# A fused token, recurrence and expert kernel on Trainium2: outputs of two expert pairs added on VectorE before the transpose, and the gate in one pass

## What is computed

```python
h = _L0_tok_ref(x, ...)                       # 1024 queries of 64 channels per batch
h = jnp.concatenate([h, txt], axis=1)         # 1152 tokens per batch
h = h + _L0_attn_ref(_layernorm(h), ...)      # recurrence over the 16 batches
h = h + _L0_ffn_ref(_layernorm(h), ...)

def _L0_ffn_ref(x, gate_w, gate_b, w1, w2, w3):
    logits = jnp.einsum('bsd,de->bse', x, gate_w) + gate_b
    top_probs, top_idx = jax.lax.top_k(jax.nn.softmax(logits, axis=-1), 2)
    top_probs = top_probs / jnp.sum(top_probs, axis=-1, keepdims=True)
    dispatch = jnp.sum(jax.nn.one_hot(top_idx, 16) * top_probs[..., None], axis=-2)
    hidden = jax.nn.silu(jnp.einsum('bsd,edh->bseh', x, w1)) * jnp.einsum('bsd,edh->bseh', x, w2)
    expert_out = jnp.einsum('bseh,eho->bseo', hidden, w3)
    return jnp.einsum('bseo,bse->bso', expert_out, dispatch)
```

## Time and profile before

| | us |
|---|---|
| median of 3 runs | 2227.41 (2227.31 to 2228.99) |
| the profiled execution's own time | 2234.98 |
| its span, first to last instruction | 2233.2 |
| PE busy | 2042.9 |
| DVE busy | 1842.9 |
| POOL busy | 1453.0 |
| ACT busy | 1121.3 |
| mean granted clock of TensorE | 0.972 |

### The profile page before, as it was taken

One profiled execution on the slowest core, in us unless ns is written; L12 is line 12 of the kernel. 1 busy time (PEld: TensorE's weight loads), 2 busy tenths in 40 slices (PEclk: granted clock), 3 DMA queues, 4 the chain that ended last, 5 costly groups with the idle time before them and its releaser, 6 DMA issues.

```text
span 2233.2 us, 42161 instructions
## 1 busy us (share of the span) xinstructions
PE 2042.9 (91%) x13857; PEld 1544.3 (69%) x13857; DVE 1842.9 (83%) x4580; ACT 1121.3 (50%) x2472; POOL 1453.0 (65%) x1657
## 2 busy tenths in 40 slices
PE   2468899999999999999999999999999999999989
PEld 1356677767677777767677776767777676777655
DVE  1336898989889898989989898998988899898886
ACT  1225455555555555555555555555545555544443
POOL 0378888577675758767575776857576785758600
PEclk9768999999999999999999999999999999999999
DMA  8787656366663647666464666646466665522200
GB/s 194 212 237 190 188 143 198 96 188 190 168 175 115 193 122 202 179 174 192 119 186 110 196 176 174 197 132 177 112 187 171 181 195 145 165 81 79 59 3 6
DMA packets 363271, 346.58 MB, mean 155 GB/s; under 512 B 49456, under 2 KB 313776, under 8 KB 362928
## 3 DMA queue, kind: packets, MB, share of 16 engines
q1 hardware_dynamic: 313904, 209.60, 34.8%
q0 software_dynamic: 49152, 134.28, 20.3%
HBM read 205.90 MB, written 137.89 MB: 154 GB/s over the span
## 4 chain that ended last, share of the span: by engine, by line
PE 78%; DVE 12%; issue 7%; ACT 2%; DMA 1%; POOL 1%; DVEq 0%; POOLq 0%; SPq 0%; ACTq 0%
PE bank_h L650 12%; PE bank_o L659 12%; PE bank_h L651 10%; PE bank_d L750 10%; PE bank_d L740 10%; PE bank_z L669 5%; PE bank_p L686 4%; PE bank_a L762 4%; DVE hid L1025 2%; PE bank_p L705 2%; DVE v_sb L1160 2%; DVE v_sb L1153 2%; PE bank_a L775 2%; PE bank_p L704 1%; PE bank_p L710 1%
## 5 line engine op out<-in xcount | busy, mean ns | idle before, releaser
L596 POOL DMA_INDIRECT gath<-table,idx x1024 | 1122.1, 1096 | 278.3 <-issue 238.6
L650 PE MATMUL bank_h<-xsplit,w 128*128 128x384 f32 x1536 | 589.6, 384 | 13.4 <-DVE hid L1025 12.4
L651 PE MATMUL bank_h<-xsplit,w 128*128 128x384 f32 x1536 | 521.0, 339 | 0.0
L834 ACT ACTIVATE silu<-bank_h 128x384 f32<-128x384 f32 x768 | 382.3, 498 | 262.1 <-PE bank_h L651 250.4
L1025 DVE TENSOR_TENSOR hid<-silu,bank_h 128x384 f32<-128x384 f32 x768 | 415.9, 549 | 58.1 <-ACT silu L834 51.7
L650 PEld LDWEIGHTS bank_h<-xsplit,w 128*128 128x128 f32 x1536 | 293.0, 191 | 113.0 <-issue 66.5
L1125 DVE TENSOR_TENSOR wsam<-gath,cw 128x1024 f32<-128x1024 f32 x256 | 312.9, 1222 | 43.9 <-PE bank_d L740 23.5
L659 PE MATMUL bank_o<-hid,w_sb 128*64 128x384 f32 x1536 | 335.2, 515 | 14.5 <-DVE scaled L1032 13.2
L616 POOL TENSOR_TENSOR lns<-lns,neghalf 128x3 f32<-128x3 f32 x96 | 88.7, 924 | 336.9 <-DVE lns L1004 335.5
L651 PEld LDWEIGHTS bank_h<-xsplit,w 128*128 128x128 f32 x1536 | 293.9, 191 | 3.2
L740 PE MATMUL bank_d<-eye,wsam 128*128 128x128 f32 x2048 | 278.1, 280 | 15.3 <-DVE wsam L1125 13.6
(11 more groups left out here) (157 smaller groups left out, 2559.8 us busy)
## 6 DMA issues: line engine op xcount, KB each, us to landing
table<-pixmaj SPq DMA_DIRECT2D x80, 1024.0 KB, 10.3
xin<-x_dram SPq DMA_DIRECT2D x256, 256.0 KB
table<-pixmaj SPq DMA_DIRECT2D x32, 960.0 KB
table<-pixmaj SPq DMA_DIRECT2D x16, 1088.0 KB
gath<-table,idx POOLq DMA_INDIRECT x1024
out_dram<-ob SPq DMA_DIRECT2D x48, 96.0 KB, 6.7
gath<-w_dram SPq DMA_DIRECT2D x4, 512.0 KB, 9.0
interp_sb<-interp_dram SPq DMA_DIRECT2D x1, 1024.0 KB, 5.0
```

The lines of the kernel that those rows point to most:

```text
L596: pool.indirect_dma_start(out=gath[buf][:, p, :, :].rearrange("p a c -> p (a c)"), out_offset=None, in_=table[par], in_offset=bass.Indirec ...
L650: mm(bank[:, 0:GC], w12[:, e, which, 0, :], xsplit[gp][:], start=True, stop=False)
L651: mm(bank[:, 0:GC], w12[:, e, which, 1, :], xsplit[gp][:], start=False, stop=True).then_inc(ready, 1)
L834: nc.scalar.activation(silu[e % 2][:], bank_h[r][:, 0:GC], ACT.Silu).then_inc(silu_done, 1)
```

## The change

Three things are changed. DVE adds the second of two neighbouring `scaled` tiles into the first after every second W (a new add of 128 x 384 whose both inputs are in SBUF, with a wait on DVE's own `eo_scaled` ahead of it), so that Z transposes two tiles in place of four. The gate weights' two parts are laid side by side, so that P7 is 3 matmuls of 32 columns in place of 6 of 16; their sum is now made by a second small add on DVE. And the strings of all engines in `ORDER` are new.

```diff
@@ Z on PE @@
-                        pe.wait_ge(eo_scaled, n + HALF)
+                        pe.wait_ge(eo_paired, (n + HALF) // 2)
                         wait(pe, mix_v, 4 * (NGRP * b + g) + 2 * half)
                         for k in range(GT):
-                            for q in range(HALF):
+                            for q in range(0, HALF, 2):
                                 last = mm(bank_z[:, 128 * k:128 * (k + 1)], scaled[(n + q) % SB][:, 128 * k:128 * (k + 1)],
-                                          eye[:], start=q == 0, stop=q == HALF - 1, is_transpose=True)
+                                          eye[:], start=q == 0, stop=q == HALF - 2, is_transpose=True)
@@ P7 on PE @@
-                            for part in range(2):
-                                last = mm(bank_p[:, NE * k:NE * (k + 1)], xsplit[gp][:, 128 * k:128 * (k + 1)],
-                                          gate_r[:, part, :], start=part == 0, stop=part == 1)
+                            last = mm(bank_p[:, 2 * NE * k:2 * NE * (k + 1)], xsplit[gp][:, 128 * k:128 * (k + 1)],
+                                      gate_r[:].rearrange("p a e -> p (a e)"), start=True, stop=True)
@@ W on DVE @@
                         tt(scaled[n % SB][:], bank_o[:, 0:GC], wide[:, q, :], ALU.mult).then_inc(eo_scaled, 1)
+                        if q % 2:
+                            dve.wait_ge(eo_scaled, n + 1)
+                            even = scaled[(n - 1) % SB]
+                            tt(even[:], even[:], scaled[n % SB][:], ALU.add).then_inc(eo_paired, 1)
@@ P7 on DVE @@
-                        link(top, tt(logit[:], bank_p[:, 0:GT * NE].rearrange("p (k e) -> p k e", k=GT),
-                                     spread(gateb[:], 1, GT), ALU.add))
+                        parts = bank_p[:, 0:2 * GT * NE].rearrange("p (k a e) -> p k a e", k=GT, a=2)
+                        link(top, tt(logit[:], parts[:, :, 0, :], spread(gateb[:], 1, GT), ALU.add))
+                        link(top, tt(logit[:], parts[:, :, 1, :], logit[:], ALU.add))
@@ ORDER, DVE's string, its first line @@
-        "efhjkkmkmnkmmknkmkmnkemkmfnhEjkFGmmknsktumkvmwnkyxzmkmAnJJJIkJJJmIkmJnIEJIFkGksmmJntJuJkJqIvewmkymJn",
+        "efhjkkmkmnkmkmnkmkmnkmkmenEfkFhGmmknsjktukmvmwnkyxzmkmAnJJJIkJJJmIkmJnIEJFkGksmmJntJuIkJJvqwIJkymJIm",
```

More of the change, by code:

```diff
@@ L192 @@
[L192 to L195, removed]
+        "aaaaaaaaaaaaaaaabbbbbbbbcdehiaaaaaaalalmmlaaalammllmmaalaabbbbbbbblcmdmellmhmilaltmumvalaalxmazJmaJl",
@@ new lines @@
+        "aBaJDIDJaDJlDJmDImDJIlDJDaJIJaalmmlJtJuKvlIJmJImxJlJzIaalaBmDJmDJIlDJaDJKDIDJbDJlDImtJmulvJIbbbbbbbJ",
+        "lJImJcmdxeJIKlJzJlIJmJImBJDlDJDIDlDJmDJDIDKmtJluJIJvlJIhmiJmJIaaJxaJIKaJzIJaaJaJaIBJDJDDIDlDJIDJKDlD",
+        "JmtJIumJvlJIJlaJImJxmJKIlJzIlJamJIJBmDaJDlJDIDalDJaDmJDKIDmtJauJlIaJlvIJamJbmbJIbbJbbbxbJcIKlJzIJlJd",
+        "mJImBJeDlDJDIDlDJmDJDIDKmtJluJIJvlJIhmiJmJIaaaJxaJIKJzaIJaaJaJIBJDJDDIDlDJKDJIDlDJmtJIumJvlJIJlaJImJ",
+        "xmJKIlJzIlJamJIJBmDaJDlDJIDalDJaDmJDKIDmtJauJlIaJlvIJamJbmbJIbbJbbbbxJcIKdlJzIJlJemJIBmDJlDJDIDlDJmD",
@@ new lines @@
+        "JDIDKmtJluJIJvlJIhmiJmJIaaJxaJIKaJzIJaaJaJaIBJDJDIDlDJIDJKDlDJmDJItmuJlvJIJlaJImJxmJKIlJzIlJamJIJBmD",
+        "aJDlJDIDalDJaDmJDKIDmtJauJlIaJlvIJamJbmbJIbbJbbbxbJcIKlJzdlJIJmJImBJeDlDJDIDlDJmDJDIDKmtJluJIJvlJIhm",
+        "iJmJIaaJxaJIKaJzIJaaJaJaIBJDJDIDlDJIDJKDlDJmDJItmuJlvJIJlaJImJxmJKIlJzIlJamJIJBmDaJDlJDIDalDJaDmJDKI",
+        "DmtJauJlIaJlvIJamJbmbJIbbJbbbxbJcIKlJzdlJIJmJImBJeDlDJDIDlDJmDJDIDKmtJluJIJvlJIhmiJmJIaaJxaJIKaJzIJa",
+        "aJaJaIBJDJDDIDlDJKDJIDlDJmtJIumJvlJIJlaJImJxmJKIlJzIlJamJIJBmDaJDlJDIDalDJaDmJDKIDmtJauJlIaJlvIJamJb",
@@ new lines @@
+        "mbJIbbJbbbbxJcIKdlJzIJlJemJIBmDJlDJDIDlDJmDJDIDKmtJluJIJvlJIhmiJmJIaaJxaJIKaJzIJaaJaJaIBJDJDIDlDJIDJ",
+        "KDlDJmDJItmuJvlJIJalJImJxmJKIlJzIlJamJIJBmDaJDlJDIDalDJaDmJDKIDmtJauJlIaJlvIJamJbmbJIbbJbbbxbJcIKlJz",
+        "dlJIJmJImBJeDlDJDIDlDJmDJDIDKmtJluJIJvlJIhmiJmJIaaJxaJIKaJzIJaaJaJaIBJDJDDIDlDJDKJDIDltJmuJImJvlJIJl",
+        "aJImJxmJKIlJzIlJamJIJBmDaJDlJDIDalDJaDmJDKIDmtJauJlIaJlvIJamJbmbJIbbJbbbbxJcIKdlJzIJlJemJIBmDJlDJDID",
+        "lDJmDJDIDKmtJluJIJvlJIhmiJmJIaaJxaJIKaJzIJaaJaJaIBJDJDDIDlDJKDJIDlDJmtJIumJvlJIJlaJImJxmJKIlJzIlJamJ",
@@ new lines @@
+        "IJBmDaJDlJDIDalDJaDmJDKIDmtJauJlIaJlvIJamJbmbJIbbJbbbxbJcIKlJzIJlJdmJImBJeDlDJDIDlDJmDJDIDKmtJluJIJv",
+        "lJIhmiJmJIaaJxaJIKaJzIJaaJaJaIBJDJDDIDlDJIDJKDlDJmtJIumJvlJIJlaJImJxmJKIlJzIlJamJIJBmDaJDlJDIDalDJaD",
+        "mJDKIDmtJauJlIavlJIJamJbmbJIbbJbbbbxJcIKdlJzIJlJemJIBmDJlDJDIDlDJmDJDIDKmtJluJIJvlJIhmiJmJIaaJxaJIKa",
+        "JzIJaaJaJaIBJDJDDIDlDJIDJKDlDJmtJIumJvlJIJlaJImJxmJKIlJzIlJamJIJBmDaJDlJDIDalDJaDmJDKIDmtJauJlIaJlvI",
+        "JamJbmbJIbbJbbbxbJcIKlJzIJlJdmJImBJlDJeDIDlDJmDJDIDKmDJltJIuJlvJhIimJmJIaaJxaJIKaJzIJaaJaJaIBJDJDIDl",
@@ new lines @@
+        "DJIDJKDlDJmDJItmuJlvJIJlaJImJxmJKIlJzIlJamJIJBmDaJDlJDIDalDJaDmJDKIDmtJauJlIaJlvIJamJbmbJIbbJbbbbxJc",
+        "IKdlJzIJlJemJIBmDJlDJDIDlDJmDJDIDKmtJluJIJvlJIhmiJmJIaaJxaJIKaJzIJaaJaJaIBJDJDDIDlDJKDJIDlDJmtJIumJv",
+        "lJIJlaJImJxmJKIlJzIlJamJIJBmDaJDlJDIDalDJaDmJDKIDmtJauJlIaJlvIJamJbmbJIbbJbbbbxJcIKlJzdlJIJmJImBJeDl",
+        "DJDIDlDJmDJDIDKmtJluJIJlvJhIimJmJIaaJxaJIKaJzIJaaJaJaIBJDJDDIDlDJKDJIDlDJmtJIumJvlJIJlaJImJxmJKIlJzI",
+        "lJamJIJBmDaJDlJDIDalDJaDmJDKIDmtJauJlIaJlvIJamJbmbJIbbJbbbxbJcIKlJzIJlJdmJImBJeDlDJDIDlDJmDJDIDKmtJl",
@@ L476, in build @@
         eo_scaled = sem("eo_scaled")
+        eo_paired = sem("eo_paired")
         mix_ready = sem("mix_ready")
@@ L1099, in run @@
                         g = args[0]
-                        top.start(b, TOP_N * g + 4)
+                        top.start(b, TOP_N * g + 5)
                         dve.wait_ge(gap_tanh, NGRP * b + g + 1)
@@ L1224 @@
 LN_N = 5
-TOP_N = 12
+TOP_N = 13
 def kernel(**inputs):
```

140 lines of the change are left out of this document (59 added, 81 removed).

## The result

The changed kernel takes 2265.59 us, median of four executions, where the kernel before takes 2228.2 us on the same chip. The ratio is 1.0158, 95% interval 1.0139 to 1.0178: slower by 1.6%. The forecast was 2264 us, within 2200 to 2300, and slower. The profiled execution took 2268.54 us with a span of 2266.7 us, and its mean granted clock is 0.951 where it was 0.972.

The account below looks back on a forecast made before the run. PE bound the kernel by 6.4 us a batch; the change would make DVE tighter by 6.3. +2.7 us over 14.8 batches is +40, -3 at the end: from 2227.4 to 2264 us, own range 2240 to 2300, 8-in-10 range 2200 to 2300.

Parts of the forecast that it names:

- The sum by place: Per batch: additions in DVE's three pauseless stretches, 6.7 us, less 2.0 for PE's lead and 2.0 for Z: +2.7 us.
- the lower bound: DVE's new add at 0.47 us, its wait on DVE's own semaphore being free, instead of the 0.60 us forecast.
- DVE's work: DVE's own time per batch rises by 7.9 us, from adds 7.2 and the gate's second add 0.7, to 125.7 us.
- The exposed part of the adds: Ten of twelve adds a batch fall where DVE has no pause; PE's 1.0 us lead hides 2.0 us a batch.
- Z: Six halved transposes a batch on PE save 0.65 us each; only three, at or in the open stretches, count: 2.0 us.
- The gate: P7 in one pass saves PE 0.3 us, the second small add costs DVE 0.24 us, each three times a batch.
- The order: New strings leave pieces mostly where they were, so the move itself costs nothing.
- The clock: Falls of TensorE's granted clock after PE's long waits, about 1.4 us each, half hidden; +5 us, left to the upper end.
- A: A 30.0 us stretch of the batch where DVE works without pause and PE waits on DVE's weights and ACT's map copies.
- The second way to the term: PE's present 4.6 us of unavoidable waits put on DVE's 125.7 us a batch: 130.3, +19 us in all, 2246 us.
- The faster one: Rival: DVE's 11.0 us of waits a batch swallow the 7.9 us added; 2178 us, half success 2202; chance 0.24.
- No change: Rival: exposed adds and PE's saving cancel, the order bringing 2.5 us a batch into open stretches; 2227 us, chance 0.12.

Follow-up runs that it names:

- the run without the wait: Changed kernel with adds of the same size and place reading constant inputs, so none waits for its forerunner: 2248.55 us, ratio 1.0079 to the kernel before.
- the old order: The ORDER strings of the kernel before; the whole new code under them took 2266.55 us, ratio 1.0171 to the kernel before.
- the filled kernels: Changed kernel and kernel before, each with unread matmuls put where PE waits: 2246.23 us (ratio 1.0078) and 2226.88 us (ratio 0.9988).

## Why the prediction was right, step by step

**The sum by place.** The total is right, and its places are not. By its own terms the forecast was about 5 us ahead of the twelve batches, 2.7 us in each of them, 32 us, and -1 us behind. Measured in the profiles: 10.3, 21.5 (1.8 us a batch; a batch is 130.6 us, forecast 131.5) and 1.7 us. That 33.5 us come out against 37 is in part luck.

**The bound.** The forecast made DVE the tighter engine by 6.3 us a batch. It is tighter by 1.1 us (123.2 against 122.1 us), PE still holds more of the chain (49% against 36%) and is the busier one from 200 to 2200 us (92.9 against 91.4%). The direction is shown, not the size: both engines are near the bound. PE's waits for DVE rose from 1.3 to 6.5 us a batch, over the 1.5 us at which I would have been wrong.

**The add.** 0.56 us long, 192 times, and start to start 1.06 us for a W with its add against 0.47 us for an instruction alone: 0.59 us, forecast 0.60. That I did not take the lower bound was right, by the run without the wait.

**DVE's work.** Forecast 125.7 us a batch, measured 123.2. This term was too large although the single add was not. The durations of DVE's groups add up to 120.3 us more than before (2132.7 against 2012.4 us), but the engine's busy time grew by 100.3 us only the earlier trace rows: overlaps between its instructions grew by 20 us. That is 1.2 us a batch, half of the 2.5 us; the rest is open. An instruction that no longer waits starts before its forerunner ends. That was in my rows, and I applied it to the add but not to the waits that go.

**The exposed part of the adds.** Forecast (6.0 for ten adds, less 2.0 for PE's lead) 4.0 us a batch, 59 us in 14.8 batches; measured 62 to 64 us in the old order. The size holds, though with the adds' falls of the clock in it, which the forecast left out. That it is a matter of ten adds and a lead of 1.0 us isn't shown by this: a share of a half, as the Z has too, tells the same sum.

**Z.** 0.65 us less each was right (62.1 us in all, forecast 62.4). Forecast to be worth three of six, 29 us; measured 29 to 31 us in the old order.

**The gate.** Forecast 0.72 x 14.8 = 11 us, measured 5 (2 to 8). L1093 lasts 0.207 us and starts 0.23 us after its forerunner, as forecast. PE's saving is 15.8 us in all, 0.33 us a gate. I gave it no value in the packed stretches, and half of it, 8 us, would explain the result; that is the term that was mis-sized. At a half for DVE's part too (11 us) the gate would have come out at -2 us, which the interval rules out: a half on either engine is no law.

**The order.** Costed at nothing; with the whole new code it is nothing that can be told, -3 us with an interval of some 6 to either side. But the reason given, that it moves little, was wrong: the same strings cost the old code 43 us. In the profiles 9 us are lost at the start and 2 of them are gained in the twelve batches; the rest is within the spread.

**The end.** -3 us forecast for the last 123 us. The profiles have +1.7 us behind the product at 2004.80 (2036.64 now), and of that +1.0 us behind the very last one, at 2129.31 (2161.79 now). Over the last 123 us PE's busy time fell from 110.84 us to 104.69, about the 6.4 us forecast (four groups of 1.6), but DVE's rose from 86.75 to 94.55 and the clock there is 0.94. Which of the two took the gain wasn't tried apart.

The last 123 us of the changed kernel, columns as in the earlier trace rows:

```profile
2143.70:2266.70 123.00, 104.69 (x512) 65.94 (x511) 94.55 (x248) 49.50 (x105) 4.25 (x5) 0.94 0.02 4
```

**The clock.** Here the prediction was right by errors that cancel. It read in the trace that a stop of PE in A is followed by a low clock, priced one fall at 1.4 us, and left it out of the sum as a possible +5 us. The falls came in every batch. In the twelve batches one lacks 3.5 us of clock time and not 1.4, and filling gives 1.5 us of it back (130.6 to 129.1), where I had counted on 0.7. From 200 to 2200 us 42.6 us more are lacking, and they cost about 15 us. Without them the change costs 20 us: 11 at the start and 0.8 us a batch (129.1 against 128.3 us in the filled kernels), and not the 2.7 us of my sum. So that sum was some 1.9 us a batch too large for what it described, and the clock and the start, which it left out or had small, made up for it. The second way to the term, unavoidable waits put on DVE's work, gave +19 us; that the number is nearly the same proves little, since its DVE work was 2.5 us too large.

**The rivals.** The faster one needed the lag to be carried past PE's lead: DVE's waits did fall, by 3.6 us a batch, and so they swallowed about half of the adds, but not more. Where both engines are near full, a wait of one isn't free room. "No change" needed the order to bring 2.5 us a batch; it brought 0.2.

## What to carry to other kernels

Where two engines are both near full (91% and 83% here) and hand work to each other, expect only part of an added or removed microsecond at the end: it was 0.54 and 0.48 here in one order, 0.40 and 0.68 in the other, and 0.8 for the wait ahead of the add. Distrust a zero sum of such parts; moving 115 us onto the one to save 62 us on the other lost here in either order. Price the granted clock with the sum and not beside it: where the change lengthens the waits of a nearly full TensorE, count the places where several stand close together. Here one such place a batch became a fall of the clock in every batch, worth 1.5 us each. A hand-made order is fitted to one code: compare code in both orders before either is judged.

## What the runs showed of the hardware

Stops of TensorE that stand close together cost more than their length. In the changed kernel it is idle for 1.94 and 1.23 us within some 4 us, after shorter stops, and the granted clock is 0.78 in the window in which they end and 0.88 in the next. With 1.47 us of matmuls without use in the first stop, the second being filled as well, it stays at 1.00, and the whole kernel is 18 us faster although PE has 280 instructions more.

On VectorE an add of 128 x 384 in fp32 that waits for its forerunner's result starts 0.03 us after that one ends, and an independent one 0.08 us before. This 0.11 us was worth 17 us over 192 adds.
